# A graph network on one core: SyncE and ScalarE fetch some of the gathered tiles row by row

## The reference

```python
h = relu(layernorm(x));  x = x + mean over edges into dst of h[src] @ W_l.T + b_l + h @ W_r.T
h = relu(layernorm(x));  x = x + relational layer: two sums of coeff[type, b] * h[src], each times W
h = relu(layernorm(x));  x = x + attention over edges: q[row] . (k[col] + edge_attr @ We), softmax per row, sum of v[col], gated
h = relu(layernorm(x));  x = x + sum over edges with this src of h[dst]
```

## Time and profile before

| | us |
|---|---|
| three runs: median (lowest to highest) | 9674.96 (9657.1 to 9678.51) |
| profiled execution: span from the first to the last instruction | 9654.6 |
| median less that span | 20.4 |
| first layer, from its first gather to its last | 2018.6 |
| second layer | 2022.9 |
| attention | 2067.4 |
| last sum | 2016.9 |

### The profile page before, as it was taken

One profiled execution on the slowest core, in us unless ns is written; L12 is line 12 of the kernel. 1 busy time (PEld: TensorE's weight loads), 2 busy tenths in 40 slices (PEclk: granted clock), 3 DMA queues, 4 the chain that ended last, 5 costly groups with the idle time before them and its releaser, 6 DMA issues. The chain is left out here.

```text
span 9654.6 us, 111112 instructions
## 1 busy us (share of the span) xinstructions
PE 5769.7 (60%) x28659; PEld 4406.5 (46%) x28659; DVE 6268.9 (65%) x14884; ACT 2670.2 (28%) x8519; POOL 6762.4 (70%) x7106
## 2 busy tenths in 40 slices
PE   5466787778784466655666566666666244444443
PEld 2144565555554344444445455555555233333333
DVE  8999788888884566666666566666666533333333
ACT  0044111111111344444443255555555100000000
POOL 0077777777776677777776677777777577777776
PEclk6555999999997677777777899999999555555555
DMA  1000333333336433333333344444444222222224
GB/s 32 14 14 14 82 92 93 92 92 92 92 90 140 85 55 55 55 55 55 55 55 36 108 111 112 111 112 112 111 111 108 49 54 54 54 54 54 54 54 60
DMA packets 1411288, 707.04 MB, mean 73 GB/s; under 512 B 1167308, under 2 KB 1271608, under 8 KB 1410536
## 3 DMA queue, kind: packets, MB, share of 16 engines
q0 software_dynamic: 254160, 559.07, 23.1%
q1 hardware_dynamic: 1156504, 140.86, 10.4%
HBM read 595.05 MB, written 104.05 MB: 72 GB/s over the span
## 5 line engine op out<-in xcount | busy, mean ns | idle before, releaser
L1534 POOL DMA_INDIRECT l_rows<-h_tab,l_index x1616 | 1530.7, 947 | 507.5 <-issue 455.3
L650 POOL DMA_INDIRECT l_rows<-h_tab,l_words x1616 | 1524.7, 943 | 515.7 <-issue 407.5
L1151 POOL DMA_INDIRECT l_rows<-h_tab,l_index x1616 | 1526.4, 945 | 506.6 <-issue 467.2
L693 PE MATMUL l_sums<-l_onehot,l_rows 128*128 128x128 f32 x3232 | 826.9, 437 | 1294.0 <-issue 1127.6
L1669 PE MATMUL l_sums<-l_weighted,l_rows 128*128 128x256 f32 x3232 | 1186.8, 531 | 647.5 <-issue 530.8
L693 PEld LDWEIGHTS l_sums<-l_onehot,l_rows 128*128 128x128 f32 x3232 | 719.7, 328 | 1401.2 <-issue 1300.4
L681 DVE TENSOR_TENSOR acc<-acc,l_sums 128x128 f32 x1616 | 463.8, 287 | 1324.0 <-PE l_sums L693 1118.6
L1548 ACT ACTIVATE l_weighted<-l_onehot,l_weights 128x128 f32<-128x128 bf16 x3232 | 987.5, 388 | 1109.6 <-DVE l_onehot L601 1045.3
L1669 PEld LDWEIGHTS l_sums<-l_weighted,l_rows 128*128 128x128 f32 x3232 | 816.7, 265 | 816.3 <-issue 551.5
L1596 DVE TENSOR_TENSOR acc<-acc,l_sums 128x256 f32 x1616 | 678.3, 420 | 677.0 <-PE l_sums L1669 523.0
L1938 POOL DMA_INDIRECT l_kv<-kv_tab,l_words x816 | 796.8, 977 | 248.6 <-issue 248.6
(11 more groups left out here) (374 smaller groups left out, 10371.5 us busy)
## 6 DMA issues: line engine op xcount, KB each, us to landing
staged<-tmp SPq DMA_DIRECT2D x195, 304.0 KB, 2.6
l_rows<-h_tab,l_index POOLq DMA_INDIRECT x3232
l_rows<-h_tab,l_words POOLq DMA_INDIRECT x1616, 2.5
by_src<-words_src SPq DMA_DIRECT2D x96, 152.0 KB, 3.3
l_kv<-kv_tab,l_words POOLq DMA_INDIRECT x816, 2.8
l_attr<-in_edge_attr SPq DMA_DIRECT2D x44, 272.0 KB, 5.0
l_kv<-kv_tab,moments POOLq DMA_INDIRECT x600
h_tab<-h SPq DMA_DIRECT2D x21, 448.0 KB, 3.0
```

What stands on the lines that cost most here:

```text
L650: pool.indirect_dma_start(rows[b][:, j, :], None, table, bass.IndirectOffsetOnAxis(ap=words[k % 3][:, at + j, 0:1], axis=0)).then_inc(rows ...
L693: done = nc.tensor.matmul(sums[q % SUMS][:, j, 0:P], rows[b][:, j, :], onehot[b][:, j, :], start=True, stop=True)
L1151: pool.indirect_dma_start(rows[b][:, j, 0:D], None, table, bass.IndirectOffsetOnAxis(ap=index[q // Q16 % WORDS][:, q % Q16 * H + j, :], ax ...
L1534: pool.indirect_dma_start(rows[b][:, j, :], None, h_tab, bass.IndirectOffsetOnAxis(ap=index[q // Q16 % WORDS][:, q % Q16 * H + j, :], axis ...
```

## The change

A class `Fetcher` fetches one tile at a time on SyncE or ScalarE, with one DMA for each of its 128 rows. Every sixteen quads (`EVERY`) it fetches the last tile of one quad: in each of the sixteen quads before, it loads eight row numbers (`LOADS`) into registers and issues eight DMAs of one row, whose address in the table is computed from a register. Two buffers take turns. `pause=2` makes it do so in every second quad only. The list of a tile's 128 row numbers is brought to one partition first: in attention and the last sum straight from the sorted edges, in the first two layers from `listed_dst`, which is computed for all listed tiles at the start of the first layer.

- SyncE fetches 24 tiles in the first layer, 24 in the second, 24 in attention and 25 in the last sum.
- ScalarE fetches 12 tiles in the first layer (one in 32 quads) and 24 in the last sum (one in sixteen quads). No quad has two fetched tiles.
- GpSimd issues one gather less in each of these quads: 1,580, 1,592, 1,592 and 1,567 instead of 1,616.
- TensorE takes the last tile of such a quad from the fetcher's buffer and waits for its rows too. In attention SyncE copies the tile with one more DMA (`lay_down`) into the place where VectorE expects it.
- Some semaphores of the first layer's phases are cleared at the end of the second layer's.

```diff
+class Fetcher:
+    def __init__(self, nc, own, engine, tag, table, width, begin, lists=None, edges=None, room=None, pause=1, row_of=None):
...
+        self.count = (TILES // 4 - 2 - begin) // self.every
+    def quad_of(self, n):
+
+        return self.begin + (n + 1) * self.every + 1
...
+    def step(self, eng, q, freed):
+
+        if q < self.begin or q - self.begin >= self.count * self.every or (q - self.begin) % self.pause:
+            return
+        n, first = (q - self.begin) // self.every, (q - self.begin) % self.every // self.pause * LOADS
+        if q == self.begin:
+            self.load_list(eng, 0)
+        if first == 0:
+            eng.wait_ge(self.listed_ready[n % 2], 16 * (n // 2 + 1))
+            if n >= 2:
+                eng.wait_ge(*freed(self.quad_of(n - 2)))
+            if n + 1 < self.count:
+                self.load_list(eng, n + 1)
+        _, rows = self.nc.values_load_multi_w_load_instructions(
+            self.listed[n % 2][0:1, first:first + LOADS], engines=(self.engine,), min_val=0, max_val=NB * P - 1,
+            skip_runtime_bounds_check_because="the sort writes row numbers below NB * P")
+        for r in range(LOADS):
+            eng.dma_start(self.rows[n % 2][first + r:first + r + 1, 0:self.table.shape[1]], self.table[bass.ds(rows[r], 1), :]).then_inc(self.rows_ready[n % 2], 16)
```

In the last sum (the second layer and attention have SyncE's fetcher alone, the first layer SyncE's and, with `pause=2`, ScalarE's):

```diff
+        by_sp = Fetcher(nc, own, ENGINE.SP, f"{tag}_sp", table, D, 0, edges=sorted_edges)
+        by_act = Fetcher(nc, own, ENGINE.Activation, f"{tag}_act", table, D, EVERY // 2, edges=sorted_edges)
...
-                    for j in range(H):
+                    for j in range(H - len(fetched_at(q))):
                         pool.indirect_dma_start(rows[b][:, j, :], None, table,
```

In the first layer, at its start, on SyncE, the row numbers of all listed tiles:

```diff
+                sp.dma_start(far_words[:], sorted_edges.rearrange("(t p) w -> p t w", p=P)[:, far:TILES:2 * EVERY, 0:2][:, 0:LISTED, :]).then_inc(far_loaded, 16)
...
+                sp.dma_start(listed.rearrange("n p -> p n"), far_index[:].rearrange("p n a -> p (n a)"), allow_slow_non_contiguous=True).then_inc(far_stored, 16)
```

In attention, on SyncE:

```diff
+                def lay_down(m):
...
+                    by_sp.wait_rows(sp, n)
+                    sp.wait_ge(msg_ready, m - 3)
+                    sp.dma_start(kv[s][:, q * Q + Q - 1, :], by_sp.rows[n % 2]).then_inc(laid_by, 16)
```

More of the change, by code:

```diff
@@ L632, in _, with load_words @@
                 blocks = tiles_of(sorted_edges, T16)
[L633 removed]
+                def load_words(k):
                     if k >= 3:
@@ L637, in _ @@
                     sp.dma_start(words[k % 3][:], blocks[k][:, :, 0:3]).then_inc(words_ready[k % 3], 16)
+                for k in range(2):
+                    load_words(k)
+                for q in range(QUADS):
+                    if q % Q16 == 0 and q // Q16 + 2 < TILES // T16:
+                        load_words(q // Q16 + 2)
+                    by_sp.step(sp, q, freed)
+            @block.scalar
+            def _(act):
+                for q in range(QUADS):
+                    by_act.step(act, q, freed)
             @block.gpsimd
@@ L688, in _ @@
                     pe.wait_ge(oh_ready, q + 1)
-                    pe.wait_ge(rows_ready[b], 16 * H * (q // RING + 1))
+                    gathered[b] += H - len(fetched_at(q))
+                    pe.wait_ge(rows_ready[b], 16 * gathered[b])
+                    of = [rows[b][:, j, :] for j in range(H)]
+                    for fetcher, n in fetched_at(q):
+                        fetcher.wait_rows(pe, n)
+                        of[H - 1] = fetcher.rows[n % 2]
                     for j in range(H):
@@ L1156, in _ @@
             def _(act):
-                for g in range(DEALS):
-                    deal.scalar(act, g)
+                for q in range(QUADS):
+                    if q < DEALS:
+                        deal.scalar(act, q)
+                    if q == by_act.begin:
+                        act.wait_ge(far_stored, 16)
+                    by_act.step(act, q, freed)
             @block.vector
@@ L1184, in _ @@
                     nc.vector.memset(rows[b][:, :, D:cols], 1.0)
+                for fetcher in (by_sp, by_act):
+                    for n in range(2):
+                        nc.vector.memset(fetcher.rows[n][:, D:cols], 1.0)
                 nc.vector.memset(acc[:], 0.0).then_inc(cleared, 1)
@@ L1221, in _ @@
                     pe.wait_ge(oh_ready, q + 1)
-                    pe.wait_ge(rows_ready[b], 16 * H * (q // RING + 1))
+                    gathered[b] += H - taken(q)
+                    pe.wait_ge(rows_ready[b], 16 * gathered[b])
+                    of = [rows[b][:, j, :] for j in range(H)]
+                    for fetcher, n in fetched_at(q):
+                        fetcher.wait_rows(pe, n)
+                        of[H - 1] = fetcher.rows[n % 2]
                     for j in range(H):
@@ L1664, in _ @@
                     pe.wait_ge(scaled, q + 1)
-                    pe.wait_ge(rows_ready[b], 16 * H * (q // RING + 1))
+                    gathered[b] += H - taken(q)
+                    pe.wait_ge(rows_ready[b], 16 * gathered[b])
+                    rows_of = [rows[b][:, j, :] for j in range(H)]
+                    if taken(q):
+                        by_sp.wait_rows(pe, by_sp.number_at(q))
+                        rows_of[H - 1] = by_sp.rows[by_sp.number_at(q) % 2]
                     for j in range(H):
@@ L1897, in attend_phase @@
         HALVES = 2 * GROUPS
+        by_sp = Fetcher(nc, own, ENGINE.SP, "l2_sp", kv_tab, 2 * D, 4, edges=by_src,
+                        room=whole[:].rearrange("p b c -> p (b c)")[:, NB * C:])
+        taken = lambda m: 0 if by_sp.number_at(m) is None else 1
+        laid_by = sem("laid_by")
+        freed = lambda m: (laid_by, 16 * (by_sp.number_at(m) + 1))
+        gathers_upto = lambda m: sum(Q - taken(n) for n in range(m % 4, m + 1, 4))
         def half(m):
@@ L1924, in _ @@
                     sp.dma_start(words[m % AHEAD], rows[m]).then_inc(words_ready[m % AHEAD], 16)
+                    lay_down(m - 4)
+                    if m == 4:
+                        sp.wait_ge(guard_ready, 1)
+                    by_sp.step(sp, m, freed)
+                for m in range(HALVES - 4, HALVES):
+                    lay_down(m)
             @block.gpsimd
```

94 lines of the change are left out of this document (80 added, 14 removed).

## The result

The changed kernel takes 9511.15 us in the median of four runs (9507.31 to 9525.65), the kernel before 9674.79 in four runs beside it (9657.1 to 9678.51). The ratio is 0.9837, with a 95% interval of 0.9823 to 0.9851: 1.6% less, clear of no change. The profiled execution is the longest of the four, 9525.65 us for a span of 9523.6, where the one of the earlier trace rows was the shortest of its four.

What follows compares the result with a forecast made beforehand. GpSimd's gather pace was taken to bound the four stages. Removing 133 gathers saves 166.9 us; plus 5 for the start and 7 for late SyncE gives −155: span 9500, time 9520 us, range 9495 to 9760.

Steps and rivals of the forecast that it cites:

- GpSimd's pace is the time of the four stages: All four gather stages: time is 1616 gathers times GpSimd's pace; 133 fewer gathers save 166.9 us if rows arrive in time.
- the 7 us for moments in which SyncE is late: Allowance added for SyncE being late in spite of its margin, as behind attribute loads of up to 2.46 us.
- A row at 0.47 us and a load at 0.64: SyncE's cost per fetched row and per eight-register load with gap: 70.4 us over sixteen quads, so every stage fits.
- A price for the extra write of a single-row DMA: SyncE's rows: sequencer's extra increment writes might cost issue time; were all of 0.567 due to it, the dearest case.
- SyncE's sharing of the DMA engines is harmless: Four stages: SyncE and ScalarE share sixteen DMA engines with GpSimd; DMA share of 0.27 to 0.44 leaves room.
- ScalarE in the first layer at nothing: First layer: ScalarE's eight rows every second quad, 4.4 us, costed at nothing; at most they take the layer's 45 us.
- The start, 5 us: First layer's start: 6,144 small pieces to load delay VectorE's first one-hot; stall of 0 to 10, taken as 5 us.
- A row of 0.50 or more: SyncE's rows: at 0.50 no change, 9671 us (chance 0.03 within 0.2%); from 0.50 on it decides whether SyncE becomes bound.
- Rows one after the other: Rival on row fetching: each row waits 2.5 us for the previous landing, 320 us a tile; called hardly likely.
- The 20.4 us between span and median: Whole kernel: median 9674.96 lies 20.4 us above the 9654.6 span; added at the end of the sum.
- the second rival: Gather stages: SyncE becomes the bound, 10518 us at 0.57 a row, about 12255 at 0.71; slower had chance 0.23.

## Why the prediction was right

The prediction was 9520 (9495 to 9760); the median is 9511.15, in the range and 9 us below the point.

- *GpSimd's pace is the time of the four stages.* Right. Compared at the same pace of 944 ns, the windows lost 39.4, 28.9, 33.8 and 58.5 us for 36, 24, 24 and 49 gathers; the terms were 45.0, 30.0, 30.7 and 61.2, and 45.0 less 5 for the start is 40.0. The predicted windows of 1973 to 1980, 1993, 2037 and 1956 became 1979.2, 1994.0, 2033.6 and 1958.4. The predicted span of 9500 became 9493.6 and 9523.6 in the two profiles, mainly by the pace. At 944 ns the span lost 161.0 us: of the 166.9, about 4.7 went to the start, and the 7 us for moments in which SyncE is late did not show.
- *A row at 0.47 us and a load at 0.64.* The sum was nearly right, its parts were not, and that their errors have opposite signs is luck. The DMA lasts 0.228, less than any DMA in the earlier trace rows, and under the 0.30 to 0.34 that I named; with register operation and gaps it is 0.416. The register load was the other way: 0.79 instead of 0.60, and 0.93 with its gaps. 128 x 0.416 + 16 x 0.93 = 68.1 us instead of 70.4, and the margins read from SyncE's waits are 3.3 to 7.1 us for sixteen quads instead of 0.5 to 4.8.
- *A price for the extra write of a single-row DMA* did not show. The Trainium skill (DMA: Bandwidth & Descriptors, "Why a DMA increments its semaphore by 16 and not by 1") says that the sequencer itself writes the increments of the engines that such a DMA does not use; that this costs issue time was my fear. At 0.228 us a row is cheaper than every DMA of the earlier trace rows, with the stores of whole tiles at 0.320 and 0.360. That a row does go through few engines is seen in the packets of ScalarE's DMA queue: 12,696 with all its rows, 9,600 without its 1,536 rows and 12 one-row lists of the first layer, so two packets for each. Whether the 0.228 us hold such a write, no run tells.
- *SyncE's sharing of the DMA engines is harmless.* Right for the rows: with all rows fetched and all gathers kept the ratio is 1.0006. The one exception is the store of the list at the start, which does hold up the gathers.
- *ScalarE in the first layer at nothing.* Nearly: without its rows 11 to 13 of the 15 us come back. Its first copy behind a block of rows comes after 3.54 us of issue, where the earlier trace rows shows 1.28 us of waiting, and it catches up in the next, which then waits for 0.58 only.
- *The start, 5 us.* 8.2 in the first profile, about 4.7 in the second. The size was luck, for the cause was wrong: I blamed the load of the far words. VectorE waited 4.3 us for that one, but the stall comes from the store of the list in 6144 pieces, as its move and its removal showed.
- *Rivals.* A row of 0.50 or more did not come, on the chips where before takes 9675. Rows one after the other: no. The bound does pass to SyncE once its quad takes longer than GpSimd's 4.8 to 4.9 us, as the runs with one tile in 14 and in 10 show; the margin was real and small.
- *The 20.4 us between span and median.* They were added without a cause. The profiled execution of the kernel before was the shortest of its runs and had 944 ns; 3 ns on 6464 gathers are 19.4, so the slower pace would account for them. That is an estimate: no profile shows the kernel before at the slower pace.
- *What I had not in the list at all:* a chip on which instructions themselves come with gaps. There the second rival came true through no price of a row that the trace of before could show.

## What to carry to other kernels

Where one engine's issue rate is the bound and others idle, work can go to them even in a much dearer form (128 row DMAs of 0.416 us in place of one gather of 1.25), as long as each of them is given less per period than the bound takes; work the period out from the pace of a whole stretch and not from single instructions, since here 0.16 us of a 4.8 us quad decided. Judge gains of some tens of microseconds by stage windows at an equal pace of the bounding instruction, not by two profiles of different executions. And a list of small numbers can go to memory in the layout in which it lies: stored so, with the strided side moved to the reads of one tile each, it left 1.2 us of waits where the store in 6144 pieces had left 5.9 to 9.7 (in the first 60 us).

## What the runs showed of the hardware

- A register load on SyncE costs by where it begins: thirteen words from word 76 of a row in 1.23 us, from word 25 in 2.94; nine from word 36 in 1.02, from word 27 in 2.13; twelve from a multiple of four in 1.01, eight in 0.79. ScalarE's loads of eight take 0.03 more. All fast ones in these runs begin at multiples of four words, 16 bytes, and all slow ones elsewhere.
- A DMA of one row with its address in a register takes SyncE 0.228 us and ScalarE 0.213; on SyncE one row follows the other every 0.416 with its register operation.
- One store in 6144 pieces of 4 bytes held up the gathers, so that three engines stood still for over ten microseconds; stored in 128 pieces the same list did not.
- The same gather takes 944 ns in some executions of the changed kernel and 947 in others, and the gathers of the sort, before any row is fetched, change with it (969 and 972). The two profiles of the kernel before both show 944; what sets the pace stays open.
- On one chip the kernel before took 18% longer (11424.88 us) at the same gather time of 944 ns and a mean clock of 0.701, with gaps ahead of instructions on all engines, and kernels with the row fetching 19 to 20% more on top. Whether that is the fetching of instructions (the instruction queue's packets went from 381 to 798 by the change) or something else there, no run here tells.
